# Two dense attentions on one Trainium2 core: the row of maxima stored first and without a cast, and own PSUM banks for the key marks in the second one

## The reference, cut to what matters

```python
attn = jnp.einsum('bnd,bmd->bnm', q * scale, k)
attn = (attn.reshape(B * nh, H, W, H, W) + rel_h[..., :, None] + rel_w[..., None, :]).reshape(B * nh, N, N)
attn = jax.nn.softmax(attn, axis=-1)
out = attn @ v
...
attn = jnp.einsum('bhnd,bhmd->bhnm', q, k) * SCALE
r_p_k = tvk[iv] + thk[ih]
attn = attn + jnp.einsum('bhnd,nmd->bhnm', q, r_p_k) * SCALE
attn = jax.nn.softmax(attn, axis=-1)
out = jnp.einsum('bhnm,bhmd->bhnd', attn, v)
```

## Time and profile before

| what | value |
|---|---|
| median of 3 runs | 6802.88 us (6791.27 to 6805.6) |
| the profiled execution | 6800.92 us |
| its span | 6799.0 us |
| busy share of the span, PE / PEld / DVE / ACT / POOL | 86% / 47% / 53% / 37% / 36% |
| DVE, maxima of L3B (L1176), 768 of them | 939.1 us, 1224 ns each |
| DVE, maxima of L0B (L1176), 768 | 935.3 us, 1222 ns each |
| ACT, exponentials (L1162), 768 in each stage | 785.3 us, 1023 ns each |
| PE, scores (L1088), 6144 matmuls in each stage | 802.2 us in L0B, 793.6 us in L3B |
| PE, marks (L1078), 1536 in each stage | 300.2 us in L0B, 298.6 us in L3B |
| PE, values of L3B (L1114), 3072 | 743.8 us |

### The profile page before, as it was taken

The page is one execution under the profiler, slowest core; times in us unless marked ns, Lnnn a source line. Parts: engine busy times, 40 slices in busy tenths (PEclk is TensorE's granted clock), DMA queues, the critical chain, the costliest instruction groups (busy, mean ns, idle before and its releaser), DMA issues. The chain is left out here.

```text
span 6799.0 us, 129026 instructions
## 1 busy us (share of the span) xinstructions
PE 5839.6 (86%) x44140; PEld 3217.6 (47%) x44140; DVE 3615.3 (53%) x5453; ACT 2516.3 (37%) x3334; POOL 2457.0 (36%) x2361
## 2 busy tenths in 40 slices
PE   8579999999977976677668879999999997879996
PEld 6553333333353343457555733333333334868885
DVE  4247777777746964434554345555555553451212
ACT  2225555555522212222221235555555552112221
POOL 0045555555514941110000144454454451053023
PEclk9789999999998997778758989999999998979998
DMA  4853434333334210000001543333333335567665
GB/s 145 266 166 89 92 90 93 91 89 89 88 75 135 87 51 4 0 1 1 1 0 49 170 129 97 102 101 97 102 102 97 102 100 195 178 229 238 210 228 185
DMA packets 839800, 741.83 MB, mean 109 GB/s; under 512 B 514933, under 2 KB 722453, under 8 KB 828726
## 3 DMA queue, kind: packets, MB, share of 16 engines
q1 hardware_dynamic: 827062, 710.76, 35.9%
q0 software_dynamic: 12288, 25.18, 1.1%
HBM read 463.94 MB, written 278.00 MB: 109 GB/s over the span
## 5 line engine op out<-in xcount | busy, mean ns | idle before, releaser
L1176 DVE TENSOR_REDUCE L3B_nmax<-L3B_R 128x1 f32<-128x1024 f32 x768 | 939.1, 1224 | 711.8 <-PE L3B_R L1078 692.8
L1176 DVE TENSOR_REDUCE L0B_nmax<-L0B_R 128x1 f32<-128x1024 f32 x768 | 935.3, 1222 | 356.6 <-PE L0B_R L1078 342.7
L1162 ACT ACTIVATE L0B_PT<-L0B_R 128x1024 f32<-128x1024 f32 x768 | 785.3, 1023 | 695.0 <-PE L0B_R L1088 667.3
L1162 ACT ACTIVATE L3B_PT<-L3B_R 128x1024 f32<-128x1024 f32 x768 | 785.3, 1023 | 580.8 <-PE L3B_R L1088 539.9
L1088 PE MATMUL L0B_R<-L0B_QS,L0B_KS 64*128 64x512 bf16 (+1 forms) x6144 | 802.2, 381 | 70.0 <-issue 35.6
L1088 PE MATMUL L3B_R<-L3B_QS,L3B_KS 64*128 64x512 bf16 (+1 forms) x6144 | 793.6, 378 | 3.4 <-DVE L3B_nmax L1176 3.4
L1114 PE MATMUL L3B_O<-L3B_PT,L3B_VA 128*64 128x512 f32 x3072 | 743.8, 605 | 0.0
L1088 PEld LDWEIGHTS L3B_R<-L3B_QS,L3B_KS 64*128 64x128 bf16 (+1 forms) x6144 | 268.1, 94 | 589.3 <-DVE L3B_nmax L1176 308.0
L1088 PEld LDWEIGHTS L0B_R<-L0B_QS,L0B_KS 64*128 64x128 bf16 (+1 forms) x6144 | 258.6, 94 | 545.0 <-issue 214.1
L1109 PE MATMUL L0B_O<-L0B_PT,L0B_VA 128*32 128x256 f32 x6144 | 419.3, 389 | 4.9 <-issue 4.7
L2874 ACT ACTIVATE L3F_hidden<-L3F_H,L3F_weights 128x256 f32<-128x256 f32 x474 | 181.4, 481 | 489.4 <-PE L3F_H L2806 489.3
(11 more groups left out here) (408 smaller groups left out, 9086.5 us busy)
## 6 DMA issues: line engine op xcount, KB each, us to landing
L3F_weights<-in_L3F_w SPq DMA_DIRECT2D x79, 1251.0 KB, 5.8
scr_sumsL<-L3B_OT SPq DMA_DIRECT2D x96, 512.0 KB
L3C_sums<-scr_sumsL SPq DMA_DIRECT2D x96, 512.0 KB, 9.1
scr_rel<-L0R_terms SPq DMA_DIRECT2D x64, 384.0 KB
L0B_raw<-scr_rel SPq DMA_DIRECT2D x192, 128.0 KB
L3B_raw<-scr_rel SPq DMA_DIRECT2D x384, 64.0 KB
scr_parts<-L0B_qk_parts SPq DMA_DIRECT2D x96, 224.0 KB, 2.7
scr_parts<-L3B_qk_parts SPq DMA_DIRECT2D x96, 224.0 KB, 2.2
```

The costliest lines, as they stand in the source:

```text
L1162: nc.scalar.activation(PT[:, (8 * u + j) % NPT, :, :], score_pair(u, j), ACT.Exp).then_inc(s_exp, 1)
L1176: nc.vector.tensor_reduce(nmax[:, u % 2, 4 * t:4 * t + 1], pair.rearrange("p j n -> p (j n)"), AX, ALU.max, negate=True).then_inc(s_mx, 1)
```

## The change

Three things are done.

1. `row` of SyncE is cut into `store_row` (the store) and `place_row` (the placing). The new order of `steps` is `store_row`, `store_parts`, `place_row`, `store_sums`, `reorder`, `place`, `load`. It holds for both stages.
2. `nmax` is bf16, and DVE transposes it straight into `MR`. The tile `NT`, the semaphore `s_mt` and the cast are gone, in both stages.
3. In L3 alone the scores use pairs 0 and 1 by turns and the marks always pair 2. Scores wait for the exponential of two steps before, marks for the maximum of the marks before. In even steps the order on TensorE is scores, marks, values; in odd steps marks, scores.

```diff
-        nmax = st.sb("nmax", [P, 2, 32])
-        NT = st.sb("max_turned", [P, 32])
+        nmax = st.sb("nmax", [P, 2, 32], BF16)
...
         def score_pair(u, j):
 
-            p = (u + 2 * j) % NR
+            p = (u + 2 * j) % NR if L0 else j % 2
             return R[:, 2 * p:2 * p + 2, :]
 
         def max_pair(u, j):
 
-            p = (u + 2 * j + 1) % NR
+            p = (u + 2 * j + 1) % NR if L0 else 2
             return R[:, 2 * p:2 * p + 2, :]
...
-            def row(H, u):
+            def store_row(H, u):
 
                 sp.wait_ge(s_mc, H + 1)
                 sp.sem_inc(s_spw, 1)
                 pos(sp, s_mr, MAXROW * H)
                 sp.sem_inc(s_spw, 1)
                 sp.dma_start(scr["max"].rearrange("o (g t n) -> (o g t) n", g=4, t=T), MR[0:P:4, :]).then_inc(s_mo, 16)
+
+            def place_row(H, u):
+
                 sp.wait_ge(s_mo, 16 * (H + 1))
...
             def steps(H, u, i):
-                nxt = ahead(H, u, i, 3, NS)
-                if nxt is not None:
-                    store_parts(nxt[0], nxt[1])
-                nxt = ahead(H, u, i, 1, NS)
-                if nxt is not None:
-                    row(nxt[0], nxt[1])
-                nxt = ahead(H, u, i, 3, NS)
-                if nxt is not None:
-                    place(nxt[0], nxt[1])
+                follows, later = ahead(H, u, i, 1, NS), ahead(H, u, i, 3, NS)
+                if follows is not None:
+                    store_row(follows[0], follows[1])
+                if later is not None:
+                    store_parts(later[0], later[1])
+                if follows is not None:
+                    place_row(follows[0], follows[1])
                 if not isinstance(H, int) or H >= 1:
                     store_sums(H - 1, u - 1)
...
                     for j in (u - 1,) if u < NS - 1 else (u - 1, u):
                         reorder(i - 1, j)
+                if later is not None:
+                    place(later[0], later[1])
                 nxt = ahead(H, u, i, 5, NS)
                 if nxt is not None:
                     load(*nxt)
...
+                    tile = max_tile(H, u, i, j)
+                    if L0:
...
                     else:
-                        scores(u, j, j % 4, j // 4)
-                    tile = max_tile(H, u, i, j)
-                    if tile is not None:
-                        pos(pe, s_exp, 8 * H + j)
-                        max_scores(max_pair(u, j), tile[0], tile[1], tile[3])
+                        if j % 2 == 0:
+                            pos(pe, s_exp, 8 * H + j - 1)
+                            scores(u, j, j % 4, j // 4)
+                        if tile is not None:
+                            pe.wait_ge(s_mx, 8 * H + j + 14)
+                            max_scores(max_pair(u, j), tile[0], tile[1], tile[3])
+                        if j % 2 == 1:
+                            pos(pe, s_exp, 8 * H + j - 1)
+                            scores(u, j, j % 4, j // 4)
...
             def copy_rows(H, u):
                 dve.wait_ge(s_mx, T * (H + 1))
-                nc.vector.transpose(NT[:, :], nmax[:, u % 2, :]).then_inc(s_mt, 1)
-                dve.wait_ge(s_mt, H + 1)
                 pos(dve, s_mo, 16 * H)
-                nc.vector.tensor_copy(MR[:, :], NT[:, :]).then_inc(s_mc, 1)
+                nc.vector.transpose(MR[:, :], nmax[:, u % 2, :]).then_inc(s_mc, 1)
```

More of the change, by code:

```diff
@@ L833, in attend @@
         s_mx = st.sem("max_taken")
-        s_mt = st.sem("max_turned")
         s_mc = st.sem("max_copied")
@@ L976, in _ @@
                 if n == 1:
-                    row(0, 0)
+                    store_row(0, 0)
+                    place_row(0, 0)
             def steps(H, u, i):
-                nxt = ahead(H, u, i, 3, NS)
-                if nxt is not None:
-                    store_parts(nxt[0], nxt[1])
-                nxt = ahead(H, u, i, 1, NS)
-                if nxt is not None:
-                    row(nxt[0], nxt[1])
-                nxt = ahead(H, u, i, 3, NS)
-                if nxt is not None:
-                    place(nxt[0], nxt[1])
+                follows, later = ahead(H, u, i, 1, NS), ahead(H, u, i, 3, NS)
[5 more added lines that the diff above has]
+                    place_row(follows[0], follows[1])
                 if not isinstance(H, int) or H >= 1:
@@ L1128, in steps @@
                         pe.wait_ge(s_mr, MAXROW * (H + 1))
-                    if isinstance(H, int) and 8 * H + j + 12 >= T * HEADS:
-                        pe.wait_ge(s_exp, 8 * H + j - 2)
-                    else:
[L1132 to L1135, removed]
-                        scores(u, j, j % 4, j // 4)
-                    tile = max_tile(H, u, i, j)
-                    if tile is not None:
-                        pos(pe, s_exp, 8 * H + j)
-                        max_scores(max_pair(u, j), tile[0], tile[1], tile[3])
+                    tile = max_tile(H, u, i, j)
+                    if L0:
+                        if isinstance(H, int) and 8 * H + j + 12 >= T * HEADS:
+                            pe.wait_ge(s_exp, 8 * H + j - 2)
+                        else:
+                            pe.wait_ge(s_mx, 8 * H + j + 13)
+                        scores(u, j, j // 2, j % 2)
+                        if tile is not None:
+                            pos(pe, s_exp, 8 * H + j)
+                            max_scores(max_pair(u, j), tile[0], tile[1], tile[3])
+                    else:
+                        if j % 2 == 0:
+                            pos(pe, s_exp, 8 * H + j - 1)
+                            scores(u, j, j % 4, j // 4)
+                        if tile is not None:
+                            pe.wait_ge(s_mx, 8 * H + j + 14)
+                            max_scores(max_pair(u, j), tile[0], tile[1], tile[3])
+                        if j % 2 == 1:
+                            pos(pe, s_exp, 8 * H + j - 1)
+                            scores(u, j, j % 4, j // 4)
                     if j % 2 == 0 and j >= 4:
```

## The result

The changed kernel takes 6697.2 us (median of 4 runs, 6693.87 to 6712.64) against 6801.5 us for the kernel before in the same session. The ratio, estimated from all executions of the session, is 0.9853, 95% interval 0.9835 to 0.9872 (the two medians alone give 0.9847). A few single executions of these kernels took 1.5 to 2.4 times as long as the others, and no time or ratio here rests on them. The changed kernel is faster, by 104 us where 127 were forecast; 6697 lies in the range given.

| stretch | before | after | measured | forecast |
|---|---|---|---|---|
| second attention (L3B) | 1702.6 us | 1610.9 us | -91.7 | -85 |
| first attention (L0B) | 1457.7 us | 1433.8 us | -23.9 | -42 |
| all the rest | | | +8.3 | 0 |

A forecast was written before the change was run, and what follows sets the result against it. TensorE was taken to bound the second attention, SyncE's list the first. Gains of 85 + 42 = 127 us off the profiled 6800.9 give 6674, and 2 us up to the runs' median 6676 us; range 6638 to 6724.

The forecast's parts named there:

- The wait for a bank in the second attention, -85: Second attention: even marks' wait for ACT's exponential goes, period 4.35 to 4.15 us, 75 us, plus hidden waits; 85 us gained.
- tile 0: Second attention, once per head: two extra waits costing about 0.17 us become hidden; 16 us at most, 11 taken.
- The round trip of the marks, 1.70 us: Second attention: marks, DVE's reduction and release take 1.70 us, fitting the 1.97 and 2.19 available between marks.
- the rival in which it grows to 2.07: Second attention: fill, reduction and release take 2.07 us, even marks wait 0.1 per period, 38 us lost; time 6714; chance 0.12.
- marks in L3B stand for DVE's reduction: Second attention: sign that the prediction is wrong, marks waiting for DVE's reduction of the marks before.
- The row first, -42: First attention: row of maxima stored first on SyncE, 15.28 to about 14.7 us per head over 77 heads; 42 us gained.
- What SyncE saves: First attention: parts store issued during the row store's 1.73 us wait, so 0.67 us per head leave SyncE's list; 0.7 taken.
- The rival in which row first gives nothing: First attention: SyncE's wait ends when transfers ahead drain, so the 0.67 us return as wait; time 6718; chance 0.14.
- The key parts, placed later: SyncE's list: key parts land 1.2 us later; a few tenths of a us per loop restart added in the first attention.
- The cast, 0 to 8 us: DVE: no cast frees 0.6 us per head in the first attention, 8 us at most beyond the 42; second attention nothing.
- the third rival: Both stages: POOL holds the bf16 transpose as it held the cast; 6853 us at a 1.9 us hold; chance 0.04.
- The pieces cancel: Whole kernel: pieces cancel or the wait on ACT is not the cause; time within 0.2% of no change; chance 0.03.

The follow-up runs named there:

- the kernel with 12 heads: The changed kernel with TensorE's loop body in the first attention unrolled to 12 heads instead of 6; 6642.9 us, ratio 0.9760 to the kernel before.
- the kernel with banks alone: The changed kernel, but odd steps of the second attention issue scores before marks again, the marks' own pair of banks kept; 6953.4 us, ratio 1.0215.
- the kernel with own banks in that stage: The changed kernel with own banks for the marks and the new order in the first attention too; 6785.1 us, ratio 0.9967.
- The kernel written out in full: The changed kernel with bodies of 48 heads for TensorE and SyncE in the first attention, without a loop; 6616.8 us, ratio 0.9718.

## Why the prediction was right, and where it was not

- **The wait for a bank in the second attention, -85.** Right in mechanism, and low by 7 us. The wait on ACT is gone, the period is 4.14 us for the 4.15 worked out, and tile 0 is hidden entirely, where 11 of 16 us were taken: 375 x 0.21 = 79 and tile 0's 16 would be 95, the far bound; 91.7 came. Of the distance to 95, most is tile 0: its longer period, 4.52 or 4.53 us, stands 82 times in the trace before and not 94, and 82 x 0.17 = 14; another 1 us was put down to the start. With the change's part alone it was 89.4.
- **The round trip of the marks, 1.70 us.** Two kernels show it bare at 1.71. With the change the gaps between marks are 2.18 and 1.96 us, so it fits; the rival in which it grows to 2.07 did not come true. The prediction named "marks in L3B stand for DVE's reduction" as a sign of being wrong, and the weight load of the marks does so: the earlier kernel's stood 0.53 us for ACT, the new one's stands 0.81 for DVE. It costs nothing, since its wait ends when the values' matmuls do; matmuls wait for DVE only at the start of the stage. A sign of that kind has to be looked for on PE, not on PEld. The room was there but thin, 0.08 us at tile 0.
- **The row first, -42.** Right in direction, 1.8 times the gain that came, and the term that was mis-sized is TensorE's pace: "TensorE needs 14.07 and every six heads its restart of about 2.7 (32.6 / 12)". The 2.7 is only the idle time that the row of waits shows. A restart costs 4.7 us, with the clock at the lower level for the work behind it, 4.9 by the kernel with 12 heads. With 14.07 + 4.9 / 6 = 14.89 in place of 14.52 the pace is the 14.91 measured, and the term 77 x (15.28 - 14.91) = 28 where 23.9 came.
- **What SyncE saves.** The forecast was that 0.67 us of issue move into a wait of 1.73, which leaves 1.06; it is 0.94. From the start of the row's store to its landing it is 2.37 us in both kernels (means of the heads in 640 to 1790 us), so the store lands no sooner and no later. The list is shorter by 1.73 - 0.94 = 0.8 us a head, near the 0.7 taken. The rival in which row first gives nothing is out. That "the bound is SyncE's list" before was half of the truth: with TensorE's restarts taken out before the change, 36.8 us came off.
- **The key parts, placed later.** No cost, as argued; placed early again, the kernel was no faster.
- **The cast, 0 to 8 us.** 3.0 in the first attention, nothing in the second. The bf16 transpose takes the 211 ns of the f32 one, so the third rival had no ground. The trace shows the hold directly. In the first attention before the change, 47 of the 96 casts began beside a running POOL instruction and took 1080 ns on average, the other 49 took 181; in the second attention it was 2 of 96. With the change 28 of the 96 bf16 transposes of the first attention began beside one, and none of the stage took more than 214 ns. With this the trace agrees with the rule of the Trainium skill that the prediction cites (SBUF — State Buffer, "Who interferes with whom").
- **The pieces cancel.** Out: alone they gave 89.4, 22.6 and 3.0 us in their stages, 115.0 together, and 115.6 in the whole change. (By medians of whole times the three give 90, 27 and 6, 124 together, against 104: the scatter of the untouched stages is in each.)

## What to carry to other kernels

Where a tile makes a round trip through another engine, first work out what TensorE does between two of them, and order its work so that each gap is longer than the trip; own banks without that order made this kernel slower. When a wait is taken away, the next limit must be priced in full: each restart left TensorE idle for about 2.8 us and cost 4.7 to 5.0, since the work behind it ran at the lower clock, which no row of waits counts. Short waits did not cost this: with 0.46 us of waiting in every period, the kernel with banks alone kept a granted clock of 1.00 in the second attention. The restart of a long loop body was such a limit here, and a longer body was a small edit.

## What the runs showed of the hardware that was not expected

The jump back in TensorE's loop of the first attention leaves it idle for 2.3 to 4.1 us each time (up to 5.0 in the kernel with own banks in that stage), with nothing that it waits for in the profile, and costs 4.7 to 5.0 us with the granted clock of about 0.56 behind it. The prologue that runs into the loop, and the loop that runs out into the epilogue, cost nothing where the body has 12 heads: the long steps there are the five between the loop's own rounds. SyncE shows a similar pause at its own restart (row stores 18.8 us apart for 13.9).

Why the jump costs this, and why the second attention's loop, also of six heads, costs nothing, was not tried, but the DMA queues of the changed kernel's trace differ in the two stages. Packets of the queue q8, of kind "instruction", 16 KB each, in the first attention (640 to 1710 us) and in the second (4100 to 5400 us):

```profile
q8 instruction: 108, 1.77, 0.7%
```

```profile
q8 instruction: 4, 0.07, 0.0%
```

In the first attention such packets come all the time, and at each of the thirteen restarts one starts within 0.3 us of the moment at which TensorE falls idle; at the restart shown above it starts at 904.8 us and takes 1.55. In the second attention they come in its first 205 us and its last 100, and not between. This fits code of TensorE that is brought in anew in every round of the first attention's loop, whose body is longer (64 matmuls of values per head for 32), and that a jump has to wait for, while the second attention's body is brought in once. The kernel written out in full has 111 such packets in the stage and no long step, so the packets alone cost nothing. It remains an inference: no run changed the length of the body in instructions and nothing else.
